# Row maxima of the cross attention: two matmuls and one VectorE reduction per two slots

## The chip, the cores and the metric

The kernel runs on one core of one Trainium2 chip. The metric is the device time of a run in microseconds (us); lower is better. The core has a matmul engine (PE, with its weight loads shown apart as PEld), VectorE (DVE), ScalarE (ACT), GpSimd (POOL), and SyncE (SP), which issues the DMAs. Each engine takes its instructions strictly in the order in which they are written; engines wait for each other on semaphores. Matmul results go to PSUM, which the program uses as eight banks of 128 partitions by 512 numbers of 4 bytes.

## The reference, cut to what matters

A decoder layer: causal self attention, cross attention over `ctx`, and a gated pair of expert layers, each followed by a layer norm. The change touches the cross attention alone: 8 batches, 16 heads of 32 numbers, 512 queries and 512 keys.

```
energy = jnp.einsum('nqhd,nkhd->nhqk', q, k)
attention = jax.nn.softmax(energy / jnp.sqrt(jnp.float32(EMBED)), axis=-1)
out = jnp.einsum('nhql,nlhd->nqhd', attention, v).reshape(N, Lq, EMBED)
return out @ Wo.T + bo
```

The softmax subtracts the maximum of each row of the scores (one row per query, over all 512 keys). The kernel computes the scores twice: once with the queries on the partitions, only to take the row maxima, and once transposed, with the maximum subtracted inside the matmul, for the exponentials.

## The kernel before, in words

The cross attention is cut into 32 groups (8 batches by 4 groups of 4 heads), and each group into 16 slots, so there are 512 slots n; slot n belongs to group n // 16, and four groups (64 slots) make a batch. Every engine walks the slots in order (`cross_slot_tensor`, `cross_slot_vector` and so on), and what stands in a slot is written by hand. One slot holds:

- on PE: the transposed scores of slot n (L1576, into bank 2 or 3, waiting for the exponentials of slot n - 2), then the work on batches that are behind (below), then the row-max matmul of slot m = n + 22 (L1547, in `cross_max`; a matmul of 512 columns), and, in some slots, work of the group: in slot 4 of a group two steps of weighted values (L1618, 16 narrow matmuls) and the column sums (L1654), in slot 9 two more steps of L1618, in slot 11 a transposition of the maxima (L1664), in slots 14 and 0 the projection of the queries (L1626, L1632).
- on DVE: in slots 5 to 8 of a group one reciprocal each (L1929), in slot 9 a product (L1934), in slot 12 part of the shift (L1944), in slot 2 part of the queries (L1917), the work on batches behind (L1958, L178, L180, L2355, L1975 and others), and last the reduction of the maxima (L1557, in `cross_max_taken`): 128 x 512 numbers out of the bank to one column of `cross_negmax`.
- on ACT: the exponential of slot n (L1839, from bank 2 or 3 into `cpt`), and layer norm, copies and gates.
- on POOL: every four slots, three times a group, an addition of 128 x 2048 numbers (L2094) that builds the sums of the exponentials. The column sums on PE (L1654) wait for the third.

The batches that are behind (`behind(n)`) bring the output projection in slots 4 to 9 and 15 to 24 of a batch (L1722 to L1724), transpositions in slots 24, 27, 31 and 33 (L1702), the gate in slots 37 to 40 (L203 to L205) and the two expert layers in slots 44 to 67 (L1749), all counted from the start of the following batch, so that the last ones fall into slots 0 to 3 of the batch after that. So slots 10 to 14 and 25 to 36 of each batch hold little for PE beyond the two score matmuls; such slots are called light here, the others full. In slots 0 to 63 no batch is behind yet.

The row-max matmuls use banks by turns: the first 22 are issued in an earlier phase, those up to m = 63 go round banks 0, 1 and 7, and from m = 64 on (`THREE_BANKS`, four groups of 16 slots; bank 7 is needed elsewhere then) round banks 1 and 0. From there PE waits, before the matmul of slot m, until the reduction of m - 2 is done (`pe.wait_ge(s.dve_max, m - 1)`), so that it can fill one bank while DVE reads the other. The maxima are made 22 slots ahead of their use.

Of the kernel before, what the change touches and what calls it, by code (L numbers as in the profile page):

```python
# [8 lines left out]
F32 = mybir.dt.float32  # L9
# [4 lines left out]
AX = mybir.AxisListType.X  # L14

BATCH, SEQ, DIM, HEADS, EXPERTS = 8, 512, 512, 16, 8
P = 128
HEAD_DIM = DIM // HEADS
TILES = SEQ // P
# [4 lines left out]
NS = NG * SLOTS  # L24
# [10 lines left out]
BANDS = (slice(0, 3, 2), slice(1, 3, 1), slice(0, 4, 3))  # L35

SELF_MAX = (0, 1, 5)
CROSS_MAX, CROSS_MAX_FIRST = (1, 0), (0, 1, 7)

SELF_LEAD, SELF_MAX_LEAD, CROSS_LEAD = 26, 25, 22  # L40

# [1 line left out]
def split_slot(n):  # L43

    return n // SLOTS, n // PER % TILES, n % PER
# [6 lines left out]
def tile_of(k):  # L52
    return slice(P * k, P * k + P)
# [19 lines left out]
class Place:  # L73


    def __init__(self, nc, start, end):
        self.nc, self.at, self.end = nc, start, end
# [8 lines left out]
class Shared:  # L86
    def __init__(self, nc, ctx):
        sb = Place(nc, CONSTANTS, OPERANDS)
        self.bank = [ctx.enter_context(nc.psum_tensor(f"bank{i}", [P, 512], F32)) for i in range(8)]
        self.ident = sb("ident", [P, P])  # L90

        late = sb.at
        self.future = sb("future", [P, SEQ], BF16)
        self.bias_end = Place(nc, late, sb.at)("bias_1_end", [P, DIM // 2])
        self.ones = sb("ones", [P, HEAD_DIM])
        self.const = ctx.enter_context(nc.semaphore("const_written"))

        self.self_done = ctx.enter_context(nc.semaphore("self_done"))
        self.memory_done = ctx.enter_context(nc.semaphore("memory_done"))
# [1415 lines left out]
SLOT_MAX, THREE_BANKS = 2 * len(EARLY_MAX), 4 * SLOTS  # L1515
# [35 lines left out]
def cross_max_taken(dve, s, sh, m):  # L1551
    gm, jm, qt = split_slot(m)
    if jm == 0 and qt == 0 and gm >= 2:
        dve.wait_ge(s.pe_sh, gm - 1)
    dve.wait_ge(s.pe_mx, m + 1)
    col = jm * TILES + qt
    dve.reduce_max(s.negmax[gm % 2][:, col:col + 1], max_bank(sh, m)[:, :], AX, negate=True).then_inc(s.dve_max, 1)  # L1557


def cross_tensor(pe, second, s, cw, sh):  # L1560
    for n in CROSS_SLOTS:
        cross_slot_tensor(pe, second, s, cw, sh, n)
    tail_tensor(pe, s, cw, sh)


def cross_slot_tensor(pe, second, s, cw, sh, n):
    g, kt, j = split_slot(n)
    if 0 <= n < NS:
        kq = s.kq[g % 3]
        if kt == 0 and j == 0:  # L1570
            pe.wait_ge(s.shift_landed[g % 3], 32 * (g // 3 + 1))
        if n >= 2:
            pe.wait_ge(s.act_exp, n - 1)
        else:
            pe.wait_ge(second.act_ms, 2 * NG)
        pe.matmul(sh.bank[2 + n % 2][:, :], kq[0:98, 1, j, tile_of(kt)], kq[0:98, 0, j, :],  # L1576
                  start=True, stop=True).then_inc(s.pe_st, 1)
    for b, slot in behind(n):
        cross_batch(pe, second, s, cw, sh, b, slot)
        cross_expert(pe, s, cw, sh, b, slot, 0)  # L1580
    m = n + CROSS_LEAD
    if SLOT_MAX <= m < NS:
        if m >= THREE_BANKS:
            pe.wait_ge(s.dve_max, m - 1)
        elif m >= SLOT_MAX + 3:
            pe.wait_ge(s.dve_max, m - 2)
        else:
            pe.wait_ge(second.dve_ms, 2 * NG)
            pe.wait_ge(second.dve_s, NG)
        cross_max(pe, s, sh, m)  # L1590
    for step in weighted_at(n):
        cross_weighted(pe, second, s, sh, step)
    cross_group(pe, s, cw, sh, g, n % SLOTS)
    for b, slot in behind(n):
        cross_expert(pe, s, cw, sh, b, slot, 1)
# [325 lines left out]
def cross_slot_vector(dve, s, sh, n):  # L1921
    g = n // SLOTS
    at = n % SLOTS
    if at == 2 and 3 <= g + 2 < NG:
        cross_query_low(dve, s, sh, 5, g + 2)
    if 5 <= at < 5 + TILES and 0 <= g - 1 < NG:
        sums = sh.bank[5][:, tile_of(at - 5)]
        dve.wait_ge(s.pe_tot, g)
        dve.reciprocal(sums, sums).then_inc(s.dve_norm, 1)  # L1929
    if at == 9 and 0 <= g - 1 < NG:  # L1930
        e = g - 1
        dve.wait_ge(s.dve_norm, (TILES + 1) * e + TILES)
        dve.wait_ge(s.act_raw, e + 1)
        dve.tensor_tensor(s.y_raw[e % 2][:, :], sh.bank[5][:, :], s.y_raw[e % 2][:, :], ALU.mult).then_inc(s.dve_norm, 1)  # L1934
    if y_part(n, Y_LOW) == NG - 1:

        dve.wait_ge(s.act_y, NG)
        dve.tensor_tensor(s.y_lo[GROUPS - 1][:, :], s.y_raw[(NG - 1) % 2][:, :],
                          s.y_hi[:, GROUPS - 1, :].bitcast(F32), ALU.subtract).then_inc(s.dve_norm, 1)
    if at == 12 and 0 <= g + 1 < NG:  # L1940
        e = g + 1
        hl = s.shift[e % 2]
        dve.wait_ge(s.act_sh, e + 1)
        dve.tensor_tensor(hl[:, 1, :].bitcast(F32R), sh.bank[5][0:PER * TILES, 0:P], hl[:, 0, :],  # L1944
                          ALU.subtract).then_inc(s.dve_sh, 1)
    for b, slot in behind(n):
        cross_batch_vector(dve, s, sh, b, slot)
    m = n + CROSS_LEAD
    if SLOT_MAX <= m < NS:
        cross_max_taken(dve, s, sh, m)  # L1950


def cross_batch_vector(dve, s, sh, b, slot):
# [523 lines left out]
```

## Time and profile before

| what | value |
|---|---|
| median of 3 runs | 1716.77 us |
| lowest and highest | 1716.08 and 1717.36 us |
| the profiled execution, its own time | 1717.48 us |
| its span in the trace | 1714.9 us |
| busy in the span: PE, DVE, ACT, POOL | 96%, 73%, 59%, 68% |
| slots 42 to 489, which issue the maxima 64 to 511 | about 921 to 1623 us |

The share of PE is time in which at least one matmul was under way. Matmuls are pipelined: one of 512 columns is shown for about 0.40 us, while the next may start 0.23 us after it. So PE can seem busy while matmuls start less often than they could, and the distance from one start to the next tells more than the busy share.

### The profile page before, as it was taken

To read this page: it belongs to the slowest core of one execution; us is meant where nothing else is said; L and a number is where in the kernel's file an instruction comes from. 1 tells how busy PE (TensorE), PEld (TensorE's weight loads), DVE (VectorE), ACT (ScalarE), POOL (GpSimd) and SP (SyncE) were. 2 spreads that over 40 slices of the span, in tenths; PEclk is the share of its full clock that TensorE was granted. 3 is DMA by queue.
4 is the path that set the end of the run, shared out by engine and by line. 5 is a ranking of instruction groups with operands and counts; after the bars stand their busy time and mean duration, and the time that the engine had idled before them with its cause. 6 is when DMAs were issued, how large, how long until landed. Compare 5 with 4: busy or idle time off the path is not lost.

```text
span 1714.9 us, 30931 instructions
## 1 busy us (share of the span) xinstructions
PE 1643.5 (96%) x10596; PEld 1118.3 (65%) x10596; DVE 1254.9 (73%) x2790; ACT 1004.7 (59%) x2010; POOL 1169.0 (68%) x967
## 2 busy tenths in 40 slices
PE   8999999999999889999998999999999999999998
PEld 5777777777777468877853556575565656656566
DVE  6777777777777567777876677868777687777745
ACT  4666666666665543333355566676666766666664
POOL 3566665666656555654467787878798787978874
PEclk8999999999999899999999999999999999999999
DMA  7665656656665455667436434525434443533210
GB/s 217 161 168 158 171 159 164 165 162 163 165 156 154 146 183 173 189 190 215 154 110 162 126 103 118 136 63 155 111 107 115 108 138 80 160 100 106 63 50 25
DMA packets 173463, 237.80 MB, mean 139 GB/s; under 512 B 22774, under 2 KB 76278, under 8 KB 173308
## 3 DMA queue, kind: packets, MB, share of 16 engines
q1 hardware_dynamic: 173308, 235.84, 49.9%
q8 instruction: 85, 1.39, 0.3%
q14 instruction: 70, 0.57, 0.1%
HBM read 92.10 MB, written 41.94 MB: 78 GB/s over the span
## 4 chain that ended last, share of the span: by engine, by line
PE 77%; POOL 10%; DVE 4%; issue 3%; DMA 3%; ACT 2%; SPq 1%; POOLq 0%; DVEq 0%; ACTq 0%
PE bank L1749 9%; PE bank L203 7%; POOL cross_added L2094 7%; PE bank L204 7%; PE bank L205 7%; PE bank L349 6%; PE bank L1576 5%; PE bank L1618 5%; PE bank L1547 5%; PE bank L403 5%; PE bank L416 4%; PE bank L1654 2%; PE bank L980 1%; PE bank L374 1%; PE bank L1006 1%
## 5 line engine op out<-in xcount | busy, mean ns | idle before, releaser
L1557 DVE TENSOR_REDUCE cross_negmax<-bank 128x1 f32<-128x512 f32 x512 | 337.7, 673 | 99.8 <-PE bank L1547 96.7
L1839 ACT ACTIVATE cpt<-bank 128x512 f32<-128x512 f32 x512 | 297.2, 593 | 139.0 <-PE bank L1576 115.6
L494 ACT ACTIVATE pt<-bank 128x256 f32<-128x256 f32 (+3 forms) x512 | 222.2, 437 | 209.2 <-PE bank L349 193.5
L2094 POOL TENSOR_TENSOR cross_added<-cross_added,cpt 128x2048 f32<-128x2048 f32 x61 | 280.1, 4591 | 14.0 <-ACT cpt L1839 13.4
L607 DVE CUSTOM_DVE_ANT_0 bank<-bank,future 128x128 f32<-128x128 f32 (+3 forms) x512 | 240.1, 489 | 64.0 <-PE bank L403 63.9
L1576 PE MATMUL bank<-cqk 98*128 98x512 f32 x512 | 224.8, 439 | 10.7 <-ACT cpt L1839 7.3
L1547 PE MATMUL bank<-cqk 96*128 96x512 f32 x512 | 215.1, 424 | 13.9 <-DVE cross_negmax L1557 11.0
L678 POOL TENSOR_SCALAR_AFFINE_SELECT pt<-pt 128x512 f32<-128x512 f32 x128 | 81.6, 638 | 214.0 <-ACT pt L494 213.9
L2094 POOL TENSOR_TENSOR cross_added<-cpt,cpt 128x2048 f32<-128x2048 f32 x32 | 146.6, 4582 | 83.7 <-ACT cpt L1839 83.7
L349 PE MATMUL bank<-qk 98*128 98x256 f32 (+2 forms) x512 | 180.2, 355 | 6.7 <-ACT pt L494 4.5
L403 PE MATMUL bank<-qk 96*128 96x256 f32 (+2 forms) x512 | 167.9, 329 | 3.9 <-DVE self_negmax L607 2.3
L1929 DVE RECIPROCAL bank<-bank 128x128 f32<-128x128 f32 x128 | 121.8, 954 | 67.2 <-PE bank L1654 67.2
L203 PE MATMUL bank<-xt_hi,w_hi 128*128 128x512 f32 x384 | 158.2, 412 | 2.5 <-DVE w_lo L566 1.9
L1576 PEld LDWEIGHTS bank<-cqk 98*128 98x128 f32 x512 | 97.0, 189 | 93.6 <-issue 39.9
L204 PE MATMUL bank<-xt_hi,w_lo 128*128 128x512 f32 x384 | 154.1, 401 | 0.0
L205 PE MATMUL bank<-xt_lo,w_hi 128*128 128x512 f32 x384 | 152.3, 397 | 0.0
L349 PEld LDWEIGHTS bank<-qk 98*128 98x128 f32 x512 | 96.3, 189 | 82.2 <-ACT pt L494 40.7
L644 DVE RECIPROCAL bank<-bank 128x128 f32<-128x128 f32 x128 | 121.9, 958 | 33.8 <-PE bank L374 33.8
L1547 PEld LDWEIGHTS bank<-cqk 96*128 96x128 f32 x512 | 95.9, 189 | 61.2 <-DVE cross_negmax L1557 39.2
L1618 PE MATMUL bank<-cpt,cv 128*32 128x512 f32 x1024 | 124.2, 603 | 0.0
L694 POOL TENSOR_TENSOR self_added<-self_added,pt 128x1024 f32<-128x1024 f32 x64 | 118.0, 1843 | 5.4
L694 POOL TENSOR_TENSOR self_added<-pt,pt 128x1536 f32<-128x1536 f32 x32 | 111.3, 3479 | 2.7
(213 smaller groups left out, 3622.4 us busy)
## 6 DMA issues: line engine op xcount, KB each, us to landing
qk<-stage SPq DMA_DIRECT2D x384, 128.0 KB, 2.4
cqk<-cstage SPq DMA_DIRECT2D x384, 128.0 KB, 2.4
scratch_memory<-memory SPq DMA_DIRECT2D x64, 256.0 KB, 3.7
ma<-scratch_memory SPq DMA_DIRECT2D x32, 512.0 KB, 4.0
raw<-in_x_t SPq DMA_DIRECT2D x32, 256.0 KB, 2.8
v<-in_x SPq DMA_DIRECT2D x32, 256.0 KB, 3.2
scratch_y_ar<-y_ar SPq DMA_DIRECT2D x32, 256.0 KB, 2.2
my_ar<-scratch_y_ar SPq DMA_DIRECT2D x32, 256.0 KB, 4.6
```

The source lines that it names most:

```text
L203: pe.matmul(out, a[0], b[0], start=first, stop=False)
L204: pe.matmul(out, a[1], b[0], start=False, stop=False)
L205: return pe.matmul(out, a[0], b[1], start=False, stop=last)
L349: pe.matmul(bank[:, 0:SEQ - q0], kq[0:98, 1, j, first:first + P], kq[0:98, 0, j, q0:SEQ], start=True, stop=True).then_inc(s.pe_st, 1)
L403: pe.matmul(bank[:, 0:max(keys, 256)], kq[0:96, 0, j, tile_of(qt)], kq[0:96, 1, j, 0:max(keys, 256)], start=True, stop=True).then_inc(s.pe ...
L607: dve.tensor_tensor_reduce(out=scores, in0=scores, in1=sh.future[:, SEQ - P * (qt + 1):SEQ], scale=-1.0, scalar=-NEG, op0=ALU.add, op1=ALU ...
L694: pool.tensor_tensor(out, old, pt[:, :, 0:SEQ - first], ALU.add).then_inc(s.pool_add, 1)
L1547: pe.matmul(max_bank(sh, m)[:, :], kq[0:96, 0, jm, tile_of(qt)], kq[0:96, 1, jm, :], start=True, stop=True).then_inc(s.pe_mx, 1)
L1557: dve.reduce_max(s.negmax[gm % 2][:, col:col + 1], max_bank(sh, m)[:, :], AX, negate=True).then_inc(s.dve_max, 1)
L1576: pe.matmul(sh.bank[2 + n % 2][:, :], kq[0:98, 1, j, tile_of(kt)], kq[0:98, 0, j, :], start=True, stop=True).then_inc(s.pe_st, 1)
L1839: act.activation(s.pt[step % 3][:, j, :], sh.bank[2 + n % 2][:, :], ACT.Exp, scale=SCALE_CROSS).then_inc(s.act_exp, 1)
L2094: pool.tensor_tensor(s.added[:, :, :], old[:, :, :], s.pt[step % 3][:, :, :], ALU.add).then_inc(s.pool_add, 1)
```

## The change

The banks 0 and 1 become the halves of one PSUM tensor of 1024 columns (`bank_pair`). For the maxima from m = 64 on, an even slot issues both m and m + 1, into banks 0 and 1, after waiting until all earlier reductions are done; the odd slots issue none. On DVE the even slot holds one reduction over both banks, 128 x 2 x 512 numbers to two columns, which waits for both matmuls; the odd slots hold none. In all 448 matmuls keep their number, and 448 reductions become 224.

```diff
-CROSS_MAX, CROSS_MAX_FIRST = (1, 0), (0, 1, 7)
+CROSS_MAX, CROSS_MAX_FIRST = (0, 1), (0, 1, 7)
...
-        self.bank = [ctx.enter_context(nc.psum_tensor(f"bank{i}", [P, 512], F32)) for i in range(8)]
+        self.pair = ctx.enter_context(nc.psum_tensor("bank_pair", [P, 1024], F32))
+        self.bank = [self.pair[:, 0:512], self.pair[:, 512:1024]]
+        self.bank += [ctx.enter_context(nc.psum_tensor(f"bank{i}", [P, 512], F32)) for i in range(2, 8)]
...
+def cross_pair_taken(dve, s, sh, m):
+    gm, jm, qt = split_slot(m)
+    if jm == 0 and qt == 0 and gm >= 2:
+        dve.wait_ge(s.pe_sh, gm - 1)
+    dve.wait_ge(s.pe_mx, m + 2)
+    col = jm * TILES + qt
+    dve.reduce_max(s.negmax[gm % 2][:, col:col + 2], sh.pair[:, :].rearrange("p (a k) -> p a k", a=2), AX,
+                   negate=True).then_inc(s.dve_max, 2)
...
     m = n + CROSS_LEAD
-    if SLOT_MAX <= m < NS:
-        if m >= THREE_BANKS:
-            pe.wait_ge(s.dve_max, m - 1)
-        elif m >= SLOT_MAX + 3:
+    if THREE_BANKS <= m < NS and m % 2 == 0:
+        pe.wait_ge(s.dve_max, m)
+        cross_max(pe, s, sh, m)
+        cross_max(pe, s, sh, m + 1)
+    if SLOT_MAX <= m < THREE_BANKS:
+        if m >= SLOT_MAX + 3:
             pe.wait_ge(s.dve_max, m - 2)
...
     m = n + CROSS_LEAD
-    if SLOT_MAX <= m < NS:
+    if SLOT_MAX <= m < THREE_BANKS:
         cross_max_taken(dve, s, sh, m)
+    if THREE_BANKS <= m < NS and m % 2 == 0:
+        cross_pair_taken(dve, s, sh, m)
```

What this does to the order on an engine shows at three places. The first is PE in the light slots 284 to 288 (slots 28 to 32 of a batch). L1576 (L1588 after the change) is the transposed scores, L1547 (L1549) the row-max matmul, L1626 (L1640) and L1632 (L1646) the projection of the queries, L1702 (L1716) the transpositions for a batch behind. Before:

```order
L1576 MATMUL bank2<-cqk2_133 128x512
L1547 MATMUL bank1<-cqk1_132 128x512
L1576 MATMUL bank3<-cqk2_133 128x512
L1547 MATMUL bank0<-cqk1_132 128x512
L1576 MATMUL bank2<-cqk2_133 128x512
L1547 MATMUL bank1<-cqk1_132 128x512
L1626 MATMUL bank5<-ident_49,x1_group_135 128x128 x4
L1576 MATMUL bank3<-cqk2_133 128x512
L1702 MATMUL bank6<-ident_49,x2_183 128x128 x4
L1547 MATMUL bank0<-cqk1_132 128x512
L1576 MATMUL bank2<-cqk0_131 128x512
L1547 MATMUL bank1<-cqk1_132 128x512
```

After the change:

```order
L1588 MATMUL bank2<-cqk2_133 128x512
L1549 MATMUL bank_pair<-cqk1_132 128x512 x2
L1588 MATMUL bank3<-cqk2_133 128x512
L1588 MATMUL bank2<-cqk2_133 128x512
L1549 MATMUL bank_pair<-cqk1_132 128x512 x2
L1640 MATMUL bank5<-ident_49,x1_group_135 128x128 x4
L1588 MATMUL bank3<-cqk2_133 128x512
L1716 MATMUL bank6<-ident_49,x2_183 128x128 x4
L1588 MATMUL bank2<-cqk0_131 128x512
L1549 MATMUL bank_pair<-cqk1_132 128x512 x2
```

The row-max matmuls of slots 285 and 287 have moved ahead of the scores of their slot, next to the one of the slot before.

The second place is DVE in slots 284 to 290. L1557 is the reduction of one bank, L1568 that of both; L2355 (L2371) and L1917 (L1931) are the subtractions for the batch behind and for the queries. Before:

```order
L1557 TENSOR_REDUCE cross_negmax1_140<-bank1 128x1
L2355 TENSOR_TENSOR x2t_lo_158<-bank6,x2t_hi_157 128x4x128
L1557 TENSOR_REDUCE cross_negmax1_140<-bank0 128x1
L2355 TENSOR_TENSOR x2t_lo_158<-bank7,x2t_hi_157 128x4x128
L1557 TENSOR_REDUCE cross_negmax1_140<-bank1 128x1
L1557 TENSOR_REDUCE cross_negmax1_140<-bank0 128x1
L1557 TENSOR_REDUCE cross_negmax1_140<-bank1 128x1
L2355 TENSOR_TENSOR x2t_lo_158<-bank6,x2t_hi_157 128x4x128
L1557 TENSOR_REDUCE cross_negmax1_140<-bank0 128x1
```

After the change:

```order
L1568 TENSOR_REDUCE cross_negmax1_140<-bank_pair 128x2
L2371 TENSOR_TENSOR x2t_lo_158<-bank6,x2t_hi_157 128x4x128
L2371 TENSOR_TENSOR x2t_lo_158<-bank7,x2t_hi_157 128x4x128
L1568 TENSOR_REDUCE cross_negmax1_140<-bank_pair 128x2 x2
L2371 TENSOR_TENSOR x2t_lo_158<-bank6,x2t_hi_157 128x4x128
L1931 TENSOR_TENSOR cstage_134<-bank5,cstage_134 128x512
L1568 TENSOR_REDUCE cross_negmax1_140<-bank_pair 128x2
```

A reduction that stood between two subtractions is gone, and one over two banks stands behind both.

The third place is PE in slots 295 to 297, where slot 297 is slot 9 of a group and holds weighted values (L1618, after the change L1632). L203 to L205 (L205 to L207) are the gate. Before:

```order
L1576 MATMUL bank2<-cqk0_131 128x512
L203 MATMUL bank6<-x2t_hi_157,gate_hi_86 8x512
L204 MATMUL bank6<-x2t_hi_157,gate_lo_87 8x512
L205 MATMUL bank6<-x2t_lo_158,gate_hi_86 8x512
L1547 MATMUL bank1<-cqk1_132 128x512
L1576 MATMUL bank3<-cqk0_131 128x512
L1547 MATMUL bank0<-cqk1_132 128x512
L1618 MATMUL bank4<-cpt0_174,cv0_177 32x512 x4
```

After the change:

```order
L1588 MATMUL bank2<-cqk0_131 128x512
L205 MATMUL bank6<-x2t_hi_157,gate_hi_86 8x512
L206 MATMUL bank6<-x2t_hi_157,gate_lo_87 8x512
L207 MATMUL bank6<-x2t_lo_158,gate_hi_86 8x512
L1549 MATMUL bank_pair<-cqk1_132 128x512 x2
L1588 MATMUL bank3<-cqk0_131 128x512
L1632 MATMUL bank4<-cpt0_174,cv0_177 32x512 x4
```

The row-max matmul that stood right ahead of the weighted values has moved ahead of the scores of slot 297.

## Rows read from the trace of the kernel before

**Rows 1.** The page: busy time by engine, and the chain's shares by engine

```profile
PE 1643.5 (96%) x10596; PEld 1118.3 (65%) x10596; DVE 1254.9 (73%) x2790; ACT 1004.7 (59%) x2010; POOL 1169.0 (68%) x967
...
PE 77%; POOL 10%; DVE 4%; issue 3%; DMA 3%; ACT 2%; SPq 1%; POOLq 0%; DVEq 0%; ACTq 0%
```

**Rows 2.** Windows of 4 us: us, busy by engine (x instructions), PEclk, DMA

```profile
1300.00:1304.00 4.00, 3.89 (x19) 2.44 (x18) 4.00 (x8) 4.00 (x9) 3.91 (x3) 1.00 0.02 4
1304.00:1308.00 4.00, 3.75 (x18) 1.99 (x20) 3.52 (x7) 3.29 (x7) 4.00 (x3) 1.00 0.18 38
```

**Rows 3.** Groups from 900 to 1690 us: busy, mean ns, idle before, releaser

```profile
L1557 DVE TENSOR_REDUCE cross_negmax<-bank 128x1 f32<-128x512 f32 x465 | 308.1, 673 | 99.8 <-PE bank L1547 96.7
...
L1547 PE MATMUL bank<-cqk 96*128 96x512 f32 x462 | 195.9, 424 | 11.6 <-DVE cross_negmax L1557 10.5 <-ACT cpt L1839 0.7
```

**Rows 4.** Waits from 900 to 1690 us: us in total, times, longest

```profile
PEld bank L1547 <- DVE cross_negmax L1557: 38.2, 86, 1.1
...
PE bank L1547 <- DVE cross_negmax L1557: 10.5, 23, 0.8
PE bank L1654 <- POOL cross_added L2094: 9.7, 9, 1.5
```

**Rows 5.** Timeline of PE in a full slot: start, us, line, [idle <-releaser]

```profile
1278.77 0.40 PE L1576 MATMUL bank<-cqk 98*128 98x512 f32 x1
1279.00 0.40 PE L1722 MATMUL bank<-wo_hi,cy_hi 128*128 128x512 f32 x1
```

**Rows 6.** Groups of VectorE kept apart by shape: a short reduction

```profile
L1990 DVE TENSOR_REDUCE gate_max<-bank 128x4 f32<-128x32 f32 x7 | 1.3, 182 | 0.6 <-PE bank L1714 0.6
```

**Rows 7.** Timeline of PE in slots 284 to 292

```profile
1299.42 0.50 PE L1547 MATMUL bank<-cqk 96*128 96x512 f32 x1 [0.33 <-DVE cross_negmax L1557]
1299.76 0.39 PE L1576 MATMUL bank<-cqk 98*128 98x512 f32 x1
...
1307.44 0.50 PE L1547 MATMUL bank<-cqk 96*128 96x512 f32 x1 [0.23 <-DVE cross_negmax L1557]
1307.87 1.92 PE L1618 MATMUL bank<-cpt,cv 128*32 128x512 f32 x16
1310.84 1.06 PE L1654 MATMUL bank<-cross_added,ones 128*32 128x512 f32 x8 [1.05 <-POOL cross_added L2094]
```

**Rows 8.** Timeline of VectorE in slots 285 and 286

```profile
1300.68 0.67 DVE L2355 TENSOR_TENSOR x2t_lo<-bank,x2t_hi 128x512 fp32r<-128x512 f32 x1
1301.28 0.67 DVE L1557 TENSOR_REDUCE cross_negmax<-bank 128x1 f32<-128x512 f32 x1
```

**Rows 9.** Timeline of PE in slot 297

```profile
1316.61 0.40 PE L1576 MATMUL bank<-cqk 98*128 98x512 f32 x1
1316.86 0.50 PE L1547 MATMUL bank<-cqk 96*128 96x512 f32 x1
1317.30 1.92 PE L1618 MATMUL bank<-cpt,cv 128*32 128x512 f32 x16
```

**Rows 10.** Timeline of POOL in slots 286 to 292

```profile
1304.90 1.30 POOL L2046 TENSOR_TENSOR cstage<-keys,cstage 128x512 fp32r<-128x512 f32 x1
1306.14 4.56 POOL L2094 TENSOR_TENSOR cross_added<-cross_added,cpt 128x2048 f32<-128x2048 f32 x1
```

**Rows 11.** Timelines of PE in slot 270 and of ACT near slot 277

```profile
1276.81 0.50 PE L1547 MATMUL bank<-cqk 96*128 96x512 f32 x1 [0.81 <-DVE cross_negmax L1557]
...
1289.20 0.82 ACT L197 ACTIVATE x<-x,ln_shift,ln_rstd 128x512 f32<-128x512 f32 x1 [4.79 <-POOL ln_shift L193]
```

**Rows 12.** Timelines of VectorE and PE in slot 42, of PE in slot 56

```profile
921.85 1.97 DVE L1557 TENSOR_REDUCE cross_negmax<-bank 128x1 f32<-128x512 f32 x3
...
921.40 0.50 PE L1547 MATMUL bank<-cqk 96*128 96x512 f32 x1
...
938.51 0.50 PE L1547 MATMUL bank<-cqk 96*128 96x512 f32 x1 [0.67 <-DVE cross_negmax L1557]
```

**Rows 13.** A window near slot 58, columns as in group 2

```profile
942.00:944.00 2.00, 2.00 (x10) 0.62 (x3) 0.46 (x1) 0.00 (x0) 0.37 (x1) 0.50 0.00 1
```

## The prediction

> **What bounds the kernel now.** I read the page first. PE is busy for 96% of the span and carries 77% of the chain, DVE 4% [rows 1]. That seems to say that only fewer matmuls could help, and the change removes none. But the busy share counts a matmul for 0.40 us while the next may start 0.23 us later, as in a full slot (1278.77, then 1279.00) [rows 5]. So I went to the windows of 4 us over slots 284 to 292, light slots: PE still shows 3.89 and 3.75 of 4 us, though with 19 and 18 matmuls where the pace of [rows 5] allows 17 of the long kind and these include cheap transpositions; DVE is busy for 4.00 and 3.52 of 4 there [rows 2]. In full slots PE is the bound; in light ones PE and DVE pass banks to and fro. The waits price that traffic: PE's weight loads waited 38.2 us for the reductions in 86 cases, of which 10.5 us in 23 cases show as idle PE [rows 4]. On the other side DVE waited 96.7 us for L1547 [rows 3], so it isn't short of time on the whole. Last, the column sums L1654 wait for POOL's third addition, 9.7 us in 9 cases [rows 4], 1.05 of it in slot 292 [rows 7].
>
> **Full slots.** 448 matmuls stay, at 0.23 us each, and half of them move one slot earlier. A slot gets 0.23 us longer and the next one 0.23 shorter. The reduction of a pair has from one even slot to the next but one to finish, and full slots are over 1.1 us long each, so two hold over 2.3 us against the pair reduction priced below; DVE's other work of those slots is there before too. I book nothing for these slots: the cover is PE's own run of gate, projection and expert matmuls. If it is gone we are in a light slot, and that is the next part.
>
> **The price of the pair reduction.** One reduction takes 673 ns for 512 columns [rows 3], one of 32 columns 182 ns [rows 6]. The slope is (673 - 182) / 480 = 1.02 ns a column, so 1024 columns take 673 + 524 = 1.20 us. The trace has no reduction over two banks. The bounds are 1.07, if the second bank costs only the 0.40 us in which PE writes one [rows 5], and 1.35, two reductions; I take 1.20, since both rows that give the slope are reductions out of PSUM. DVE saves 1.35 - 1.20 = 0.15 us a pair, 224 times, or 33 us, as a sum of durations. In a full queue the saving is smaller: L2355 starts at 1300.68 and the next reduction at 1301.28, so one instruction holds the queue for 0.60 us, not 0.67 [rows 8].
>
> On this the Trainium skill, page Perfetto Trace Analysis, section Optimizing Scalar/DVE Operations, has two rules that pull apart. Grouping into larger operations can improve throughput if the engine is saturated; but where it isn't and causes bubbles elsewhere, breaking instructions up may let work complete sooner. It gives about 125 ns of overhead for a DVE operation on PSUM, by which the saving would be an estimated 224 x 0.125 = 28 us of DVE's time. The first rule is the faster rival below, the second speaks for my forecast.
>
> **Light slots.** Before, PE fills one bank while DVE reads the other. Now both are filled, then both are read, and nothing of the two overlaps. The loop of a pair is: from the end of a reduction to the start of the matmul 0.05, to the start of the second 0.34, as from 1299.42 to 1299.76 after a wait [rows 7], that matmul 0.40 [rows 5], DVE's start 0.04, the reduction 1.20. That is 2.03 us for two slots at best (0.04 and 0.05 are taken from the ends and starts in [rows 7, 8]: a reduction starts and is taken up with next to no gap). Other DVE work fits into the 0.8 us in which DVE waits for the matmuls, if it is ready and no longer than that. Two subtractions L2355 in a row are 1.2 us, so one loop takes 2.4, and one more takes 2.4 through the projection L1632 on PE. Before, the four pairs from slot 284 to slot 292 took 1307.44 - 1299.42 = 8.02 us [rows 7], 2.0 a pair. Now they take 2.05 + 2.4 + 2.4 + 2.0 = 8.85. And the first of them starts later: the pair of slot 282 is reduced only after L178 and L180, to about 1300.15, against the matmul at 1299.42 before. So the matmuls of slot 292 start at 1300.2 + 8.85 = 1309.05, 1.6 us late; with the second one (0.34) the weighted values start about 1.9 us late.
>
> **What is late next** is POOL. It runs without a gap from L2046 at 1304.90 through L2094, which starts at 1306.14 and takes 4.56 us [rows 10], and L1654 starts at 1310.84 after 1.05 us of idle PE [rows 7]. Matmuls overlap at their ends, so some 1.25 us can be absorbed. Left at L1654 are 1.9 - 1.25 = 0.65 us; but the matmul of slot 293 is done by then, which gives back 0.23: 0.42.
>
> **Slot 9 of a group.** In slot 297 the last L1547 sits between the scores (1316.61) and the weighted values (1317.30), 0.69 us, because it waits for a reduction that stands behind a reciprocal [rows 9]. Now it is issued in slot 296, before the scores, at 0.23, and the values follow the scores after some 0.34, the step between two matmuls of different kinds after a wait [rows 7]: 0.57 in all. Saved 0.12; 0.42 - 0.12 = 0.30. Slot 281 gives about as much.
>
> **Slots 266 to 276** are the other light stretch. PE already waits 0.81 us in slot 270 [rows 11]. Three loops (slots 266, 268, 270) bring PE to slot 272 about 0.6 us late. At the projection the pair reduction stands behind L1958, L178 and L1917, and the sums in slot 276 come about 0.8 late. ACT then absorbs most: its exponential for slot 276 stands behind L197, which waited 4.79 us for POOL, to 1289.20 [rows 11], and POOL isn't later than before. I carry 0.3 us over; it is the start from which the numbers for slots 280 to 292 above were made, so it isn't added again.
>
> So a batch of 64 slots loses 0.30 us. Slots 64 to 489 span seven batches: 7 x 0.30 = 2.1 us.
>
> **The first batch, slots 42 to 63**, has no batch behind and is light throughout. PE in slot 42 must now wait for the reduction of m = 63. That is the first of three that start at 921.85 and take 1.97 together, so it ends near 922.5, while PE started at 921.40 before [rows 12]. Five loops follow, and the sums in slot 52 come 1.5 us late. In slots 53 to 57 it turns: PE waited there behind reciprocals, 0.67 us in slot 56 alone [rows 12], and with one reduction fewer between them and one wait fewer the weighted values come 0.85 earlier. 1.5 - 0.85 = 0.65 at slot 58; with the matmul shared out, 0.6 stays.
>
> **Sum:** 2.1 + 0.6 = 2.7 us on the profiled execution's 1717.48, which is 0.7 above the median; on the median 1716.77 + 2.7 = **1719.5 us**. A measurement of this kernel can tell about 0.2% from no change, 3.4 us, so 1713.4 to 1720.2 counts as the same. Forecast: the same within that, on the slow side. With the reduction at 1.35 instead of 1.20, four to five loops a batch add 0.15 each, 0.65 x 7 = 4.6, so 1724; at 1.07 they take as much away, but only until POOL is the bound, 1716.
>
> **Rivals.**
> 1. *The unhidden loop, slower.* Place: slots 284 to 292. If the loop is 0.15 to 0.2 us longer than I have it, by the reduction or the semaphores, nothing is left of POOL's 1.25 us to take it up, and each batch pays it in full: 0.30 + 0.7 to 0.9, seven times, plus 0.6, is 7.5 to 9 us: 1724 to 1726. It decides from a loop of 2.2 us on. For it: PE already loses all of its slack over POOL in my own sum. Against it: the rows on either side of a wait show hardly a gap.
> 2. *The clock, slower.* In slots around 58, after sparse matmuls, PE was granted 0.50 of the clock for a whole window [rows 13], that is 1.2 instead of 2.4 GHz. Light stretches get sparser now. A spell of about 3.4 us as there would hold PE for up to 1.7 us more, once a batch: 7 x 1.7 + 2.7 = 15 us, 1731. Against it: the stretches at 1300 to 1308 have 1.00 with 18 and 19 matmuls in 4 us [rows 2], and lose only a tenth of these.
> 3. *DVE was the bound, faster.* In slots 284 to 292 it is busy for 7.5 of 8 us [rows 2]. If its queue sets the pace rather than the turns at the banks, five pairs a batch save 0.07 to 0.15 each, the waits behind reciprocals in slots 281 and 297 go (0.12 to 0.3 each), and POOL's wait hides the rest: 0.6 to 0.9 a batch, 4 to 6 us, 1711 to 1713. This is the first rule of the page named above. Against it: the subtractions are few, and without them DVE waits for PE.
>
> **Chances.** My forecast (1716 to 1722) 0.60, of which 0.44 is within 0.2% and 0.16 beyond it; the unhidden loop 0.17; the clock 0.08; faster 0.15, of which 0.04 within 0.2%. That is faster 0.11, same 0.48, slower 0.41. The range goes from 1714.5 to 1727: it leaves out the clock and the greater part of the faster case, under 2 in 10.
>
> **What would show it.** DVE busy falls by some 33 us, with 224 reductions near 1.20 us. In slots 284 to 292 the matmul pairs start 2.0 to 2.4 us apart, and PE's waits for the reductions grow in number of us (10.5 before [rows 4]) while they vanish behind reciprocals. L1654 in slot 36 of a batch waits hardly at all for POOL. A batch, slot 256 to slot 320, is 0.3 us longer. The forecast is wrong if the reduction takes over 1.3 us, if PEclk falls in light slots, or if L1654 still waits a microsecond for POOL, which would mean that PE had arrived on time.

## The result, and the profile after it

The changed kernel took 1731.45 us (median; 1728.45 to 1738.94), the kernel before 1716.42 beside it: a ratio of 1.0089, 95% interval 1.0068 to 1.0110. It is slower by 15 us. I had forecast 1719.5 and a range up to 1727, so both the forecast and its range are wrong. The profiled execution took 1730.33 us with a span of 1728.5, 13.6 more than the span before.

The page of the changed kernel, its busy row, its clock row, the chain by engine and the two groups that the change is about:

```profile
PE 1647.7 (95%) x10596; PEld 1127.4 (65%) x10596; DVE 1242.0 (72%) x2566; ACT 1012.2 (59%) x2010; POOL 1167.8 (68%) x967
...
PEclk9999999999999789999998999999999999999999
...
PE 80%; DVE 10%; DMA 3%; issue 3%; ACT 2%; POOL 2%; SPq 1%; POOLq 0%; DVEq 0%; ACTq 0%
...
L1568 DVE TENSOR_REDUCE cross_negmax<-bank_pair 128x2 f32<-128x1024 f32 x224 | 271.9, 1214 | 130.3 <-PE bank_pair L1549 130.2
...
L1549 PE MATMUL bank_pair<-cqk 96*128 96x512 f32 x476 | 162.7, 418 | 35.7 <-DVE cross_negmax L1568 33.4
```

Against [rows 1]: DVE has 224 instructions less and is busy for 12.9 us less, yet its share of the chain went from 4% to 10% and POOL's from 10% to 2%. That is the result in one line. DVE has no more work; PE now waits for it, and so no longer for POOL. A reduction over 1024 columns takes 1214 ns. (The transposed scores are L1588 now, the weighted values L1632, the column sums L1668.)

The waits of the changed kernel from 900 to 1700 us (total, times, longest):

```profile
DVE cross_negmax L1568 <- PE bank_pair L1549: 130.2, 134, 2.2
...
PEld bank_pair L1549 <- DVE cross_negmax L1568: 58.4, 65, 1.4
...
PE bank_pair L1549 <- DVE cross_negmax L1568: 33.4, 48, 0.9
...
PE bank L1668 <- POOL cross_added L2110: 0.9, 2, 0.6
```

Idle PE before the row maxima went from 10.5 us in 23 cases to 33.4 in 48 [rows 4], and DVE waits longer for PE too, 130.2 us against 96.7 [rows 3]. PE's wait for POOL before the column sums fell from 9.7 us to 0.9 [rows 4]. PE and VectorE both wait more: what each did beside the other they now do in turn.

Where the time lies I took from the starts of the transposed scores, one per slot. For the profiled executions, in us:

| stretch | before | changed |
|---|---|---|
| up to slot 0 | 860.5 | 861.8 |
| slots 42 to 64 | 28.38 | 29.61 |
| 64 to 128 | 101.32 | 104.42 |
| 128 to 192, 192 to 256, 256 to 320 | 101.85 101.86 101.84 | 102.59 102.57 102.61 |
| 320 to 384, 384 to 448 | 101.84 101.83 | 103.99 104.15 |
| 448 to 511 | 92.69 | 93.88 |

Three batches are 0.73 us longer and equal to each other within 0.04. Two more are 2.15 and 2.32 longer, though they run the same program. Something comes on top there that the order of the instructions doesn't explain. It is the clock. Windows of 4 us of the changed kernel, the first two at the slots of the light stretch in batch 256, the next two at the same slots one batch later (us; PE, PEld, DVE, ACT, POOL busy; granted clock; DMA):

```profile
1305.40:1309.40 4.00, 2.33 (x12) 1.42 (x10) 3.26 (x5) 3.50 (x8) 3.67 (x6) 1.00 0.01 2
1309.40:1313.40 4.00, 3.58 (x17) 2.49 (x18) 3.11 (x5) 2.91 (x6) 4.00 (x2) 1.00 0.01 2
1408.00:1412.00 4.00, 2.71 (x14) 1.67 (x12) 3.23 (x6) 3.45 (x8) 3.67 (x6) 1.00 0.02 4
1412.00:1416.00 4.00, 3.45 (x14) 2.93 (x15) 2.83 (x4) 2.97 (x7) 4.00 (x2) 0.66 0.01 2
```

PE is busy for 2.33 and 2.71 of 4 us, where the rows of before had 3.89 and 3.75 at such places [rows 2]. In the last window the mean granted clock is 0.66: for a part of it PE ran at 1.2 GHz instead of 2.4. The records give the spell as 3.4 us long, and the program falls back by 1.05 us in it (0.37 us of the batch's excess arises earlier, around slot 341, at full clock). In the next batch the spell lies around slot 400 and costs 1.6:

```profile
1490.00:1491.60 1.60, 0.66 (x3) 0.26 (x2) 1.29 (x2) 1.08 (x2) 1.60 (x1) 1.00 0.05 10
1491.60:1495.00 3.40, 3.40 (x12) 2.70 (x12) 1.37 (x2) 1.08 (x2) 3.07 (x6) 0.53 0.55 159
```

The first pair of windows shows that such a sparse stretch isn't always followed by a spell. The kernel before had no spell between slots 64 and 511 in its one profile.

### The profile page after: what moved, and what is told of

It reads as the page before. It is cut to its first block, busy times and chain, and to the rows that moved or that the text cites. A ratio compares the mean times of both kernels' runs of the same rounds, so it can differ in the third digit from the quotient of the medians.

```text
span 1728.5 us, 30903 instructions
## 1 busy us (share of the span) xinstructions
PE 1647.7 (95%) x10596; PEld 1127.4 (65%) x10596; DVE 1242.0 (72%) x2566; ACT 1012.2 (59%) x2010; POOL 1167.8 (68%) x967
## 4 chain that ended last, share of the span: by engine, by line
PE 80%; DVE 10%; DMA 3%; issue 3%; ACT 2%; POOL 2%; SPq 1%; POOLq 0%; DVEq 0%; ACTq 0%
PE bank L1763 9%; PE bank L205 7%; PE bank L206 7%; PE bank L207 7%; PE bank L351 6%; PE bank L1632 6%; PE bank_pair L1549 6%; PE bank L1588 5%; PE bank L418 5%; DVE cross_negmax L1568 4%; PE bank_pair L405 3%; PE bank L1668 2%; PE bank L376 2%; PE bank L405 2%; PE bank_pair L982 1%
## 5 line engine op out<-in xcount | busy, mean ns | idle before, releaser
L1568 DVE TENSOR_REDUCE cross_negmax<-bank_pair 128x2 f32<-128x1024 f32 x224 | 271.9, 1214 | 130.3 <-PE bank_pair L1549 130.2
L1588 PE MATMUL bank<-cqk 98*128 98x512 f32 x512 | 221.6, 442 | 9.6 <-ACT cpt L1853 9.4
L1549 PE MATMUL bank_pair<-cqk 96*128 96x512 f32 x476 | 162.7, 418 | 35.7 <-DVE cross_negmax L1568 33.4
L609 DVE CUSTOM_DVE_ANT_0 bank_pair<-bank_pair,future 128x128 f32<-128x128 f32 (+3 forms) x342 | 163.8, 489 | 42.9 <-PE bank_pair L405 42.9
L205 PE MATMUL bank<-xt_hi,w_hi 128*128 128x512 f32 x384 | 158.1, 412 | 1.3 <-DVE w_lo L568 0.7
L1588 PEld LDWEIGHTS bank<-cqk 98*128 98x128 f32 x512 | 97.5, 191 | 88.7 <-issue 42.8
L1943 DVE RECIPROCAL bank<-bank 128x128 f32<-128x128 f32 x128 | 115.8, 938 | 49.9 <-PE bank L1668 49.9
L207 PE MATMUL bank<-xt_lo,w_hi 128*128 128x512 f32 x384 | 151.7, 395 | 0.0
L646 DVE RECIPROCAL bank<-bank 128x128 f32<-128x128 f32 x128 | 121.9, 958 | 34.4 <-PE bank L376 34.4
L1549 PEld LDWEIGHTS bank_pair<-cqk 96*128 96x128 f32 x476 | 85.0, 192 | 74.8 <-DVE cross_negmax L1568 58.4
L1632 PE MATMUL bank<-cpt,cv 128*32 128x512 f32 x1024 | 124.5, 604 | 0.0
L405 PE MATMUL bank_pair<-qk 96*128 96x256 f32 (+2 forms) x342 | 112.3, 329 | 4.8 <-DVE self_negmax L609 2.5
```

The lines of the kernel that those rows point to most:

```text
L205: pe.matmul(out, a[0], b[0], start=first, stop=False)
L207: return pe.matmul(out, a[0], b[1], start=False, stop=last)
L1549: pe.matmul(max_bank(sh, m)[:, :], kq[0:96, 0, jm, tile_of(qt)], kq[0:96, 1, jm, :], start=True, stop=True).then_inc(s.pe_mx, 1)
L1568: dve.reduce_max(s.negmax[gm % 2][:, col:col + 2], sh.pair[:, :].rearrange("p (a k) -> p a k", a=2), AX, negate=True).then_inc(s.dve_max, 2)
L1632: done = pe.matmul(sh.bank[4][rows_of(j), :], s.v[g % 2][:, kt, rows_of(j)], s.pt[step % 3][:, j, :], start=(kt == 0), stop=(kt == TILES - ...
```

## The experiments

I had three suspects: the light slots, where writing and reading no longer overlap; the full slots, which I had booked at nothing; and the clock.

**Pairs in the full slots alone, and in the light slots alone.** `full_only` issues singly wherever a slot is light:

```
+def light(n):
+    return n < BATCH_SLOTS or 10 <= n % BATCH_SLOTS < 16 or 26 <= n % BATCH_SLOTS < 38
+def paired(m):
+    return not light(m - CROSS_LEAD)
...
-    if THREE_BANKS <= m < NS and m % 2 == 0:
-        pe.wait_ge(s.dve_max, m)
-        cross_max(pe, s, sh, m)
-        cross_max(pe, s, sh, m + 1)
+    if THREE_BANKS <= m < NS:
+        if not paired(m):
+            pe.wait_ge(s.dve_max, m - 1)
+            cross_max(pe, s, sh, m)
+        elif m % 2 == 0:
+            pe.wait_ge(s.dve_max, m)
+            cross_max(pe, s, sh, m)
+            cross_max(pe, s, sh, m + 1)
...
```

VectorE gets the same two cases, and the single matmuls keep the banks that they had before.

> Pairs only in full slots; the light slots (0 to 63, and 10 to 15 and 26 to 37 of each batch) keep one matmul and one reduction a slot, as before the change. If the loss comes from the light slots (the turns at two banks, or the clock there), a batch takes 101.85 us as before or 0.1 to 0.4 less, and the time is within 1 us above and 3 us below the kernel before, 1713.5 to 1717.5. If the wide reduction or two matmuls in a row cost something by themselves, a batch is longer here too, and the time lies 3 us or more above.

Measured: 1719.22 us (1714.13 to 1722.36), ratio 1.0005, interval 0.9985 to 1.0025: not told from no change, though the median lies above the 1717.5 that I had as the upper end. The five batches without a spell are 101.83 to 101.87 long, as before. But "nothing" is a sum of two things. From slot 20 to slot 26 of a batch it gains 0.5 us, behind the reciprocals and in slot 25, and from slot 44 to 46 it loses 0.41 again. Its profile also has spells at half clock from 992.5 (3.4 us) and 1606.9 (6.8 us), both in the light stretch that begins at slot 26 of a batch, where this kernel issues singly. So a spell doesn't need pairs in the light slots.

`light_only` is the reverse, from slot 128 on:

```
 def paired(m):
-    return not light(m - CROSS_LEAD)
+    return m - CROSS_LEAD >= 2 * BATCH_SLOTS and light(m - CROSS_LEAD)
```

> Pairs only in the light slots from slot 128 on, single matmuls and reductions elsewhere. If the turns at the banks in light slots are the cause, each of the batches from slot 128 to 383 loses 0.7 to 1.2 us (0.73 in the changed kernel, which also had the small gain behind reciprocals), and batches with a spell at half clock 2 us or more: 4.5 to 12 us in all. If the loss belongs to the full slots, nothing is lost: within 1 us of the kernel before.

Measured: 1726.41 us (1723.65 to 1734.06), ratio 1.0064, 1.0039 to 1.0088. Undisturbed batches are 102.54 to 102.57, that is 0.70 over the kernel before, and those from 320 and 384 take 103.93 and 104.06, with a spell of 3.4 us each, as in the changed kernel. Pairs in 18 light slots out of 64 bring nearly the whole length of an undisturbed batch, and spells at the same two places (a third, from slot 93, comes before its pairs begin). Pairs in the full slots add 0.03 us, again as a sum: at slot 44 `light_only` is 0.71 us late and the changed kernel only 0.35, at slot 46 they are 0.70 and 0.75.

**The gate slots.** Where do the 0.41 us at slots 44 to 46 come from? Timelines of PE and VectorE of the changed kernel at slots 300 and 301 (start, us, line, [idle <-releaser]):

```profile
1328.29 0.48 PE L1588 MATMUL bank<-cqk 98*128 98x512 f32 x1
...
1329.08 0.39 PE L1763 MATMUL bank<-exp_hi,x2t_lo 128*128 128x512 f32 x1
1329.61 0.73 PE L1549 MATMUL bank_pair<-cqk 96*128 96x512 f32 x2
...
1330.65 0.39 PE L1588 MATMUL bank<-cqk 98*128 98x512 f32 x1
...
1328.33 1.23 DVE L1568 TENSOR_REDUCE cross_negmax<-bank_pair 128x2 f32<-128x1024 f32 x1 [1.32 <-PE bank_pair L1549]
1329.47 0.18 DVE L2006 TENSOR_REDUCE gate_max<-bank 128x4 f32<-128x32 f32 x1
```

The pair of slot 298 is written just before slot 300, its reduction ends at 1329.56, and the pair of slot 300 waits for that: 0.30 us pass from the last expert matmul's expected successor (1329.31 at a pace of 0.23) to 1329.61. The kernel before, in the same slot, found its bank free and had no wait:

```profile
1321.55 0.39 PE L1749 MATMUL bank<-exp_hi,x2t_lo 128*128 128x512 f32 x1
1321.77 0.40 PE L1547 MATMUL bank<-cqk 96*128 96x512 f32 x1
```

`gate_single` issues singly in these six slots and in pairs elsewhere:

```
 def paired(m):
-    return not light(m - CROSS_LEAD)
+    return not 42 <= (m - CROSS_LEAD) % BATCH_SLOTS < 48
```

> The changed kernel, but with one matmul and one reduction a slot in slots 42 to 47 of a batch. If the pair reduction costs 0.4 us where it meets the gate's small operations on VectorE (slots 44 and 45), a batch without a clock spell takes 102.2 us against 102.6 in the changed kernel and 101.85 before; if that shift has another cause (the state in which the light slots leave the engines), it stays at 102.6.

Measured, in one execution: 1722.07 us, batches of 102.20 to 102.35 against 102.57 to 102.61. Its timeline of PE over the same slots, 4.2 us earlier in the span:

```profile
1324.09 0.48 PE L1593 MATMUL bank<-cqk 98*128 98x512 f32 x1
...
1325.11 0.40 PE L1554 MATMUL bank_pair<-cqk 96*128 96x512 f32 x1
...
1325.81 0.39 PE L1593 MATMUL bank<-cqk 98*128 98x512 f32 x1
```

Slot 301 starts 1.72 us after slot 300, not 2.36. Part of that is only the second matmul's 0.23, which slot 302 gives back. Net, the step from 44 to 46 shrinks from 0.41 to 0.01, and a batch gets 0.2 to 0.4 us shorter, so the wait of a pair in the gate slots is shown. One execution doesn't say what it is worth in the total. It does say something on the clock: there is no spell after slot 64 in it, though its light slots hold the same pairs as in the changed kernel. Its span is 5.4 us longer than that of the kernel before.

**The clock.** If sparse light slots cost the clock, added matmuls should bring it back. The next two kernels do all the work of the changed one and add zeros to an accumulation in 64 even light slots, from slot 42 on (the trace shows each such matmul as two records):

```
+def filler(pe, s, sh, n, times):
+    g, at = divmod(n, SLOTS)
+    if SLOTS < n < NS and light(n) and n % 2 == 0 and not 4 <= at < 10:
+        v = s.v[(g if at >= 10 else g - 1) % 2]
+        pe.wait_ge(s.zeroed, 1)
+        for _ in range(times):
+            pe.matmul(sh.bank[4][:, 0:SEQ // 2], s.zero[:, :], v[:, 0:2, :], start=False, stop=False,
+                      skip_group_check=True)
...
+        filler(pe, s, sh, n, 3)
         pe.wait_ge(s.dve_max, m)
```

> The changed kernel with three more matmuls of 256 columns in each even light slot outside slots 4 to 9 of a group, ahead of PE's wait for the reduction. They add zeros to bank 4. If spells at half clock come from sparse matmuls and cost the greater part of the 15 us, none is left from slot 16 on, the batches are all alike (102.6 us or somewhat more, by what the fillers take), the four timed runs lie close together and the time is 1722 to 1727. If the loop at the banks is all of the loss, the time is 1731 or more, since fillers only add work.

Measured: 1757.01 us, ratio 1.0231 (1.0194 to 1.0268), far above what I expected. No spell at half clock between slots 64 and 511, mean granted clock 0.990 over four executions, but batches of 107.7: three fillers at a time don't fit into PE's waits, and their price buries what the clock gives. So one at a time (`filler(pe, s, sh, n, 1)`):

> The changed kernel with one filling matmul of 256 columns in each even light slot outside slots 4 to 9 of a group, a third of filler3's. It adds zeros to bank 4. One fits into the time in which PE waits for the pair reduction, so a batch without a spell costs 102.6 to 103.6 us. If more matmuls keep the clock up, the mean granted clock is 0.983 to 0.990, between the changed kernel and filler3 (0.990); if the clock does not depend on them it is as in after_again.

Measured: 1728.61 us (1726.59 to 1730.88), ratio 1.0056 (1.0037 to 1.0076). No spell after slot 64, and batches of 103.30. Windows at the slots of the spell above, 3.1 us earlier in the span:

```profile
1404.90:1408.90 4.00, 3.94 (x20) 3.03 (x20) 3.23 (x7) 3.00 (x7) 3.67 (x6) 1.00 0.01 2
1408.90:1412.90 4.00, 3.51 (x20) 2.56 (x19) 3.23 (x4) 3.46 (x7) 4.00 (x2) 1.00 0.02 4
```

PE is busy for 3.94 of 4 us where it was 2.71, and the clock stays at 1.00. The batches of this kernel are 0.7 us longer than the changed kernel's undisturbed ones, and still it takes less time: 3 us less than the changed kernel's first runs and 6 less than the runs beside it, which come next. The intervals of the ratios overlap at their edges; over all executions, the second set of this kernel below among them, ten with one filler average 1727.8 us and eight without 1733.5.

**The changed kernel again**, on the same chip as `filler1`:

> The changed kernel once more, beside the kernel before on this chip, for the mean granted clock of its executions. If sparse light slots lower the clock, its mean lies at 0.976 to 0.982 against about 0.986 before; if the clock of the first runs (0.973 to 0.982) was chance, it lies at 0.984 to 0.988 and the time falls to 1722 to 1725. Its batches without a spell take 102.6 us again.

Measured: 1734.64 us (1728.68 to 1740.04), ratio 1.0090 (1.0065 to 1.0115). Batches without a spell are 102.56 and 102.57 long again. Its mean granted clock is 0.978 over four executions, as in the first four. The spells of its profile lie at the same two kinds of place, from slot 14 and from slots 30 and 31 of a batch, five of 3.4 us and in the last batch one of 10.2.

**The same fillers in the kernel before**, to take the clock out of the comparison:

```
         if m >= THREE_BANKS:
+            filler(pe, s, sh, n, 1)
             pe.wait_ge(s.dve_max, m - 1)
```

> The kernel before with the same added matmul of zeros as filler1 (one of 256 columns in each of the same even slots of the light stretches; nothing is left out). It asks what the difference between the two kernels is when both keep the clock. If the clock is the larger part of the change's loss: the kernel before had few spells to lose (mean granted clock .986 over 42 executions, none between slots 64 and 511 in the profile), so the added matmuls are nearly pure cost here, at most 0.71 us a batch as in the changed kernel (102.59 to 103.30), 5 us in all, less where PE waits anyway: 1717.7 + 3 to 5 = 1721 to 1723, and the changed kernel with them stands only 5 to 7 us above it. If the loop is the larger part and the clock a small one, the gap stays near the 15 us that the two kernels have without the added matmuls: this kernel then comes out near 1714, with a batch no longer than 101.84.

> The changed kernel with one added matmul of zeros, once more, on the chip of the run above: 1728.6 as measured first (1726.6 to 1730.9), clean batches of 103.3 us and no spell at half the clock between slots 64 and 511. By the clock theory 5 to 7 us above the kernel before with the same matmuls, by the loop theory 13 to 15.

Measured on one chip: 1717.62 us (1712.95 to 1721.85) and 1727.57 (1724.06 to 1730.17), 9.95 apart. That lies between the theories' 5 to 7 and 13 to 15. The reason is the fillers' own price. In the changed kernel they add 0.76 us to a batch (102.59 to 103.35), in the kernel before mostly 0.19 (101.84 to 102.03; one batch has 102.20). There the shift is 0.43 at slot 20 of a batch and 0.0 at slot 22, behind the column sums, where PE waited for POOL anyway; the changed kernel has used up that wait. Seven times the 0.57 of difference is 4.0 us. Without it, and with no spell after slot 64 in either, the changed kernel is 6 us behind, and 9 of the 15 us are left for the clock. Both are estimates: the prices come from single profiles, and the 15 us have an interval of 12 to 19.

**One reduction for each bank, with both matmuls still in the even slot.** This keeps the half of the change that moves matmuls and undoes the one that joins the reads:

```
     if THREE_BANKS <= m < NS and m % 2 == 0:
-        pe.wait_ge(s.dve_max, m)
+        pe.wait_ge(s.dve_max, max(m - 1, THREE_BANKS))
         cross_max(pe, s, sh, m)
+        pe.wait_ge(s.dve_max, m)
         cross_max(pe, s, sh, m + 1)
...
-        cross_pair_taken(dve, s, sh, m)
+        cross_max_taken(dve, s, sh, m)
+        cross_max_taken(dve, s, sh, m + 1)
```

> Two matmuls in even slots as in the changed kernel, but two single reductions, and the first matmul waits only for bank 0, the second for bank 1. PE writes one bank while VectorE reads the other again. If the lost overlap of writing and reading is the cause, the light slots lose little: a batch at 101.8 to 102.3 us, 1716 to 1720. If the order on PE (nothing in odd slots, two in even ones) is the cause, it costs as the changed kernel does, 102.6 us a batch and 1725 to 1731.

> The kernel with two matmuls in even slots and two single reductions again, on this chip. If writing beside reading is worth what the first run says, 101.2 us a batch against 101.85, it is 4 to 6 us faster than before: a ratio of 0.9965 to 0.998. If the first run was a matter of the clock, the ratio is 0.999 to 1.001.

Measured: 1712.45 us, ratio 0.9973 (0.9948 to 0.9997), and on another chip 1713.59, ratio 0.9982 (0.9965 to 0.9999). Both intervals end just below 1. It beats both kernels, though it has all 448 reductions; I had expected only that it loses little (101.8 to 102.3 a batch). Undisturbed batches are 101.15 to 101.17, 0.69 shorter than before (one in the first profile has 101.41). First the changed kernel in slots 284 to 292, pairs and then VectorE:

```profile
1307.46 0.73 PE L1549 MATMUL bank_pair<-cqk 96*128 96x512 f32 x2 [0.93 <-DVE cross_negmax L1568]
...
1309.58 0.73 PE L1549 MATMUL bank_pair<-cqk 96*128 96x512 f32 x2 [0.92 <-DVE cross_negmax L1568]
...
1311.90 0.73 PE L1549 MATMUL bank_pair<-cqk 96*128 96x512 f32 x2 [0.24 <-DVE cross_negmax L1568]
...
1314.24 0.62 PE L1549 MATMUL bank_pair<-cqk 96*128 96x512 f32 x2
...
1316.35 0.73 PE L1549 MATMUL bank_pair<-cqk 96*128 96x512 f32 x2 [0.19 <-DVE cross_negmax L1568]
1317.01 1.92 PE L1632 MATMUL bank<-cpt,cv 128*32 128x512 f32 x16
1318.75 1.04 PE L1668 MATMUL bank<-cross_added,ones 128*32 128x512 f32 x8
...
1308.30 1.23 DVE L1568 TENSOR_REDUCE cross_negmax<-bank_pair 128x2 f32<-128x1024 f32 x1 [0.70 <-PE bank_pair L1549]
```

Then the kernel with two reads, the same slots:

```profile
1291.99 1.10 PE L1549 MATMUL bank_pair<-cqk 96*128 96x512 f32 x2 [0.47 <-DVE cross_negmax L1559]
...
1293.40 1.07 PE L1549 MATMUL bank_pair<-cqk 96*128 96x512 f32 x2
...
1295.77 1.10 PE L1549 MATMUL bank_pair<-cqk 96*128 96x512 f32 x2
...
1291.27 1.27 DVE L1559 TENSOR_REDUCE cross_negmax<-bank_pair 128x1 f32<-128x512 f32 x2
1292.45 0.27 DVE L1959 TENSOR_TENSOR cross_shift<-bank,cross_shift 16x128 fp32r<-16x128 f32 x1
1292.65 1.27 DVE L1559 TENSOR_REDUCE cross_negmax<-bank_pair 128x1 f32<-128x512 f32 x2
```

In the changed kernel DVE's reduction starts at 1308.30, after both matmuls, and the next pair at 1309.58, after the reduction; 0.92 us of PE are lost in between. With two reads the first matmul of a pair starts at 1291.99 while DVE is still in the second of the two reductions that began at 1291.27, and the reductions from 1292.65 on begin while the pair from 1291.99 (until 1293.09) is being written. Which part of the 0.69 us comes from which slots I can read off the shifts against the kernel before: 0.58 in slots 20 to 22 and 0.9 in slots 36 to 38, where the weighted values and the column sums follow, against 0.4 and 0.75 lost in the light slots ahead of them. Why a pair there is worth more than two singles in two slots I didn't separate further.

## Why the prediction was wrong

**Bounds.** That full slots are PE's and light slots a turn of two engines held. DVE's 130.2 us of waits show that it wasn't the bound, and the rival *DVE was the bound* is out.

**The price of the reduction** held: 1.20 us forecast, 1.214 measured. DVE busy fell by 12.9 us, not 33. The page counts time in which two records overlap once, and they do overlap: a subtraction booked with 0.67 us holds the queue for 0.60 [rows 8], and so does a single reduction booked with 673 ns (1301.28 to 1301.88), while a pair is booked with 1214 ns and holds it for 1.14 (1308.30 to 1309.44). A pair saves 0.06 us of the queue, 224 times 13 us. I took the sum of durations, 2 x 0.673 - 1.20, for the fall in busy time, although I had said beside it that the saving in a full queue is smaller.

**The light slots** held closely. Four pairs from slot 284 to 292 were to take 8.85 us and took 8.89 (1307.46 to 1316.35), in steps of 2.12, 2.32, 2.34 and 2.11. POOL ended at 1318.14 and L1668 started without a wait at 1318.75, so POOL's slack was used up as worked out; the shift carried into slot 28 was 0.23 to 0.27 us (forecast 0.3), at slot 36 1.73 to 1.78 (forecast 1.6), and at slot 38, behind the column sums, 0.45 to 0.49 (forecast 0.42). The rival *unhidden loop* needed a loop of over 2.2 us without a subtraction in it, and did not come.

**Full slots: "I book nothing for these slots"** failed, by 0.41 us a batch. The step argued that two full slots hold over 2.3 us and the reduction takes 1.2. But that compares lengths and not instants: the reduction can't start before the second matmul, and in slots 44 to 46 the next pair asks for the banks 1.0 us after that. At slot 44 the changed kernel is 0.32 to 0.37 us late, which is what I had for the whole batch; at slot 46 it is 0.73 to 0.79, and stays there. I had counted what the full slots give back (slots 281 and 297) and not what they take. So an undisturbed batch costs 0.73 us and not 0.30. The last batch costs 1.19 in the profile: its maxima end at slot 489, and from there on the shift stays (1.63 at slot 36, 1.57 at slot 37, where the other batches fall back to about 0.7); I had booked it as the others. Six batches and the last are 5.6 us, not 2.1. With the first batch, whose own share I can't tell from its spells, this is about the 6 us that remain at equal clock. It gives some 1722 to 1723 us, within my range, on the slow side.

**The clock** is the larger failure, by the estimate above 9 us of 15. I described this rival rightly in its mechanism (a spell of about 3.4 us in a light stretch, up to 1.7 us each; measured 1.05 and 1.6) and gave its time as 1731, which is the measured one. That the number fits is in part luck: it was made of a spell of 1.7 us in each of seven batches and 2.7 us for the rest, while the profile has spells in three of the seven and some 6 us for the rest. I gave it a chance of 0.08 and left it out of the range. The argument was that windows with 18 and 19 matmuls have clock 1.00 and "lose only a tenth of these". That was the step that failed: such windows now have 12 and 14, because two waits of 0.9 us come one behind the other in slots 284 and 286. My own loop of 2.05 us with two matmuls and the scores in it said so; I replayed where instructions start and never counted what is left in a window. And the clock isn't confined to the changed part. Over 60 executions of the kernel before the mean granted clock runs from 0.979 to 0.991, and the time with it, about 1.2 us less for each 0.001 more (9 executions at 0.980 to 0.983 average 1722.2 us, 14 at 0.989 or more 1713.8). The changed kernel's mean of 0.978 against 0.987 is worth about 10 us by that, a second route to the same share.

Neither route says that the change brought all of it. In the two profiles of the changed kernel the spells between slots 64 and 511 cost 5.4 and 8.5 us, by what their batches take over undisturbed ones. Part of the lower mean clock lies before slot 0, where both kernels run the same instructions: in the first profile of the changed kernel 37.5 us passed there at half clock, against 27.3 in the kernel before, and over all twelve profiles it is 17.1 to 41.0. So the mechanism is shown (spells in the light stretches, and none after slot 64 in the three profiles of the changed kernel with fillers), but its size only to a few us.

**The spread.** I took 0.2% for what can be told from no change, from three runs that agree within 0.1%. The 60 executions reach from 1711 to 1728 us.

On joining reads: the Trainium skill, page Perfetto Trace Analysis, section Optimizing Scalar/DVE Operations, advises larger operations where the engine is saturated and smaller ones where it isn't but causes bubbles elsewhere. Here DVE is busy for 73% of the span, and the runs bear out the second half: one read per pair 1.0089, two reads 0.9973 and 0.9982 with the same matmuls in the same slots. The same page, section Optimizing Tensor Performance, says that independent matmul groups should rotate through different PSUM banks so that reading one out overlaps the next group's matmuls. The changed kernel keeps two banks but reads them as one, and its trace shows the overlap gone: 33.4 us of idle PE before the row maxima against 8.4 with two reads. Two rows of the waits of that kernel from 900 to 1700 us, and its group of L1549 over the same stretch:

```profile
DVE cross_negmax L1559 <- PE bank_pair L1549: 81.1, 92, 1.9
...
PEld bank_pair L1549 <- DVE cross_negmax L1559: 37.7, 88, 1.5
```

```profile
L1549 PE MATMUL bank_pair<-cqk 96*128 96x512 f32 x455 | 160.8, 419 | 12.2 <-DVE cross_negmax L1559 8.4
```

## What to carry to other kernels

Two banks that are written together and read by one instruction are one buffer: the saving on the reading engine is 0.06 us a pair here, the lost overlap up to 0.9 us of PE. When a change makes a stretch sparser for PE, put a price on a spell at half clock there and carry it in the range, before you add up the rest: the loop's own instants already show how little PE will do in it. And a stretch where the schedule "has room" needs the instants of write, read and next write, not the sum of their lengths; moving the matmuls alone, with a read for each bank, was the part worth having.

## What I had not expected of the hardware

A spell at 0.50 of the clock came in some batches and not in others with the same program and nearly the same busy time (2.33 of 4 us with the clock kept, 2.71 with the clock lost right after). What decides between them stays open: no run here was made to vary it, and `gate_single`, with the same pairs in its light slots, had none. All 16 spells after slot 64, in six of the twelve profiles, begin in slots 14, 29, 30 or 31 of a batch. In the kernel with two reads a spell came too, in batch 256, in each of its two profiles at the same place (1.5 us), though it is the fastest of all. Twelve executions of the kernel before with the 64 added matmuls (128 records in the trace) took 1717.62 us against 1716.12 without, interval of the ratio 0.9998 to 1.0022: that is 12 ns a record if it is anything. Here they are nearly free, but the same matmuls cost 0.76 us a batch in the changed kernel.
